# Keys, queries and the product with the convolved rows by high and low parts (three float32r products each) in the third layer of a four-layer kernel

## What is computed

```python
# third layer: B, H, W = 32, 56, 56; C = 96, 6 heads of 16, windows of 7 x 7 (49 tokens), 8 windows in a row
xn = (x - mu) * rsqrt(var + EPS) * norm_gamma + norm_beta
shifted = roll(xn, (-3, -3), (1, 2))
dw = conv_general_dilated(shifted, dw_w, 7x7, feature_group_count=C) + dw_b    # depthwise
qkv = win_partition(shifted) @ qkv_w.T + qkv_b                                 # q, k, v
attn = softmax(q * scale @ k.T + rpb + mask)
out = attn @ v + win_partition(dw)
out = out @ proj_w.T + proj_b
return x + roll(win_reverse(out), (3, 3), (1, 2))
```

## Time and profile before

| | us |
|---|---|
| median of 3 runs (lowest to highest) | 12334.83 (12328.66 to 12345.21) |
| the profiled execution | 12346.31 |
| its span, first to last instruction | 12344.5 |
| PE busy | 11557.4 (94%) |
| PE weight loads busy | 7528.1 (61%) |
| ACT busy | 7537.9 (61%) |
| DVE busy | 7030.2 (57%) |
| POOL busy | 1543.8 (13%) |

### The profile page before, as it was taken

The page is one execution under the profiler, slowest core; times in us unless marked ns, Lnnn a source line. Parts: engine busy times, 40 slices in busy tenths (PEclk is TensorE's granted clock), DMA queues, the critical chain, the costliest instruction groups (busy, mean ns, idle before and its releaser), DMA issues. The chain is left out here.

```text
span 12344.5 us, 381409 instructions
## 1 busy us (share of the span) xinstructions
PE 11557.4 (94%) x153876; PEld 7528.1 (61%) x153876; DVE 7030.2 (57%) x12108; ACT 7537.9 (61%) x12498; POOL 1543.8 (13%) x2308
## 2 busy tenths in 40 slices
PE   6999998899999999999998999998999999999999
PEld 3434443566666666666675667666666666666666
DVE  4444444556556555555446666666555555555555
ACT  4555554566566566566435777776666666666666
POOL 0000000222222222222000000000111111111111
PEclk9999999899999999999999999999999999999999
DMA  1111111122222222222463333333000000000000
GB/s 56 37 36 39 40 39 34 37 46 46 45 45 46 46 44 47 44 47 45 153 216 69 76 75 76 75 75 66 21 21 21 21 21 21 22 21 21 22 21 20
DMA packets 1104420, 602.40 MB, mean 49 GB/s; under 512 B 864651, under 2 KB 1076566, under 8 KB 1099704
## 3 DMA queue, kind: packets, MB, share of 16 engines
q1 hardware_dynamic: 1091496, 553.66, 19.0%
q10 hardware_dynamic: 12288, 38.54, 0.9%
HBM read 308.38 MB, written 282.75 MB: 48 GB/s over the span
## 5 line engine op out<-in xcount | busy, mean ns | idle before, releaser
L950 PEld LDWEIGHTS banks<-L_ident,L_PR 113*113 113x113 f32 x9216 | 1104.5, 180 | 415.6 <-issue 290.1
L1264 DVE COPY L_VB<-banks 49x384 f32<-49x384 f32 x512 | 287.3, 561 | 1859.4 <-PE banks L966 1859.4
L1026 PE MATMUL banks<-L_XN,L_W 97*128 97x392 f32 x3072 | 1249.0, 516 | 13.2 <-DVE L_XN L1339 0.7
L1185 ACT ACTIVATE L_PR<-L_SX 113x588 f32<-113x588 f32 x1536 | 1084.3, 706 | 277.0 <-DVE L_SX L1301 270.5
L950 PE MATMUL banks<-L_ident,L_PR 113*113 113x113 f32 x9216 | 1249.1, 272 | 2.5 <-ACT L_PR L1185 1.8
L1295 DVE TENSOR_REDUCE L_MX<-banks 113x12 f32<-113x588 f32 x1024 | 783.4, 765 | 605.3 <-PE banks L988 605.3
L1169 ACT COPY L_PT<-banks 113x452 f32<-113x452 f32 x1792 | 871.1, 528 | 395.3 <-PE banks L950 395.2
L378 PE MATMUL banks<-scan_XS,scan_W1T 97*96 (+1 forms) x2688 | 1110.2, 551 | 0.0
L1103 PE MATMUL banks<-L_Hd,L_W 128*97 128x392 f32 x3072 | 1097.2, 493 | 0.0
L1005 PE MATMUL banks<-L_VB,L_PT 113*49 113x34 f32 x36864 | 1074.0, 214 | 2.5 <-ACT L_PT L1169 1.0
L1005 PEld LDWEIGHTS banks<-L_VB,L_PT 113*49 113x49 f32 x36864 | 1026.1, 127 | 26.9 <-issue 1.3
(11 more groups left out here) (199 smaller groups left out, 20433.5 us busy)
## 6 DMA issues: line engine op xcount, KB each, us to landing
L_X<-after_L SPq DMA_DIRECT2D x768, 147.0 KB
after_L<-L_X SPq DMA_DIRECT2D x512, 147.0 KB
conv_T<-L_norm_by_phase SPq DMA_DIRECT2D x96, 512.0 KB, 3.3
L_norm_by_phase<-L_XP SPq DMA_DIRECT2D x512, 84.0 KB, 2.2
scan_XT<-in_x SPq DMA_DIRECT2D x33, 1176.0 KB, 7.0
L_norm<-L_XA SPq DMA_DIRECT2D x256, 147.0 KB, 2.0
L_conv<-conv_D ACTq DMA_DIRECT2D x96, 392.0 KB, 3.0
L_XR<-L_norm SPq DMA_DIRECT2D x256, 147.0 KB, 2.2
```

The lines of the kernel that those rows point to most:

```text
L950: mm = pe.transpose(bank(TURN[a])[0:SPAN, (k % 4) * SPAN:(k % 4 + 1) * SPAN], PR[:, st.v if lag else st.u, 2 * k:2 * k + 2, :].rearrange(" ...
L1026: pe.matmul(bank((7, 6, 7)[j])[:, 0:CH], W1[0:C + 1, j * 128:(j + 1) * 128], XN2[:, st.u], start=True, stop=True).then_inc(s[f"fc1_{j}"], 1)
L1185: act.activation(PR[:, u, a, 0:TOK], SX[:, u, a], ACT.Exp).then_inc(s[f"probs{half}"], 1)
```

## The change

In the L2 pass keys, queries and the product with the convolved rows are made in the manner of `conv_pass`. The three weight tiles are split once, ahead of the pass, into a high part and the rest by VectorE (`split_weights`, a block of its own). In each step POOL splits XN of the next chunk into XNH and XNL behind its copy (`to_windows`), and DW of the same chunk into DWH and DWL (`split_convolution`). `by_parts` on PE adds the three products. Values, scores, transposes, heads and `project` stay as they were, and values still read XN. `front` waits for `xn_parts` where it waited for `xn`, `project_convolution` for `dw_parts` where it waited for the load, and the load of DW for `dw_parts` where it waited for `proj`. DWH and DWL have the layout of DW and are read in the same order as DW was.

```diff
+def split_weights(nc, name, parts):
+    with semaphores(nc, name) as sem:
+        rounded = sem("rounded")
+        with nc.Block() as block:
+            @block.vector
+            def _(dve):
+                for whole, high, low in parts:
+                    dve.tensor_copy(high.bitcast(F32R), whole).then_inc(rounded, 1)
+                dve.wait_ge(rounded, len(parts))
+                for whole, high, low in parts:
+                    dve.tensor_tensor(low.bitcast(F32R), whole, high, ALU.subtract)
...
+        if kind == "L2":
+            split_weights(nc, "L2_parts", [(t[0:C + 1], h[0:C + 1], l[0:C + 1]) for t, h, l in ((Wq, WqH, WqL), (Wk, WkH, WkL), (Wp, WpH, WpL))])
...
                     if kind == "L2":
-                        st.wait("proj", lag + 4)
+                        st.wait("dw_parts", lag + 4)
...
+                def by_parts(out, wh, wl, xh, xl, stop=True):
+                    for n, (wt, xt) in enumerate(((wh, xh), (wh, xl), (wl, xh))):
+                        mm = pe.matmul(out, wt.bitcast(F32R), xt.bitcast(F32R), start=(n == 0), stop=(n == 2) and stop)
+                    return mm
...
-                    pe.matmul(bank(K_BANK)[0:C, 0:CH], Wk[0:C + 1, :], XN[:, st.u], start=True, stop=True).then_inc(s["k"], 1)
+                    out = bank(K_BANK)[0:C, 0:CH]
+                    if not mlp:
+                        by_parts(out, WkH[0:C + 1, :], WkL[0:C + 1, :], XNH[:, st.u], XNL[:, st.u]).then_inc(s["k"], 1)
...
                 def project_convolution(st):
-                    st.wait_turn(loaded[st.of4(1)], 1, N_LOADS, 4)
-                    pe.matmul(bank(PROJ_BANK)[0:C + 1, 0:CH], Wp[0:C, :], DW[:, st.of4(1)].rearrange("c p i j -> c i j p"), start=True, stop=False)
+                    st.wait("dw_parts", 1)
+                    raster = lambda t: t[:, st.v].rearrange("c p i j -> c p (i j)").rearrange("c p n -> c n p")
+                    by_parts(bank(PROJ_BANK)[0:C + 1, 0:CH], WpH[0:C, :], WpL[0:C, :], raster(DWH), raster(DWL), False)
...
                 def front(st):
-                    st.wait("xn", 0)
+                    st.wait("xn_parts", 0)
...
                         pool.tensor_copy(seen(XN[0:C, u]), win(XR[:, u])).then_inc(s["xn"], 1)
+                        st.wait("q", lag + 2)
+                        hold(pool, s["xn"], st.value(lag), passed)
+                        pool.tensor_copy(XNH[:, u].bitcast(F32R), XN[:, u]).then_inc(s["xn_high"], 1)
+                        hold(pool, s["xn_high"], st.value(lag), passed)
+                        pool.tensor_tensor(XNL[:, u].bitcast(F32R), XN[:, u], XNH[:, u], ALU.subtract).then_inc(s["xn_parts"], 1)
+                    def split_convolution(st):
+                        st.wait("proj", 2)
+                        hold(pool, loaded[st.of4(0)], (st.t // 4 + 1) * (16 * N_LOADS), passed)
+                        pool.tensor_copy(DWH[:, st.u].bitcast(F32R), DW[:, st.of4(0)]).then_inc(s["dw_high"], 1)
+                        hold(pool, s["dw_high"], st.value(0), passed)
+                        pool.tensor_tensor(DWL[:, st.u].bitcast(F32R), DW[:, st.of4(0)], DWH[:, st.u], ALU.subtract).then_inc(s["dw_parts"], 1)
                     def step(st):
                         if not st.static or st.t + 1 < NCH:
                             to_windows(st, -1, st.v)
+                        if st.f:
+                            split_convolution(st)
```

More of the change, by code:

```diff
@@ L724, in window_pass @@
         if kind == "L2":
+            XNH = sb("XNH", [C + 1, 2, CH]); XNL = sb("XNL", [C + 1, 2, CH])
+            WqH = sb("WqH", [128, C]); WqL = sb("WqL", [128, C]); WkH = sb("WkH", [128, C]); WkL = sb("WkL", [128, C])
+            WpH = sb("WpH", [128, C + 1]); WpL = sb("WpL", [128, C + 1])
+            DWH = sb("DWH", [C, 2, PHASES, WS, JW]); DWL = sb("DWL", [C, 2, PHASES, WS, JW])
             XR = sb("XR", [C, 2, CH]); DW = sb("DW", [C, 4, PHASES, WS, JW])
@@ L799, in window_pass @@
         if kind == "L2":
-            names += ["biased0", "biased1"]
+            names += ["biased0", "biased1", "xn_high", "xn_parts", "dw_high", "dw_parts"]
         if kind == "L3":
@@ L952, in turn @@
                     mm.then_inc(s[f"turned{a}"], 1)
+                def by_parts(out, wh, wl, xh, xl, stop=True):
+                    for n, (wt, xt) in enumerate(((wh, xh), (wh, xl), (wl, xh))):
+                        mm = pe.matmul(out, wt.bitcast(F32R), xt.bitcast(F32R), start=(n == 0), stop=(n == 2) and stop)
+                    return mm
                 def keys(st):
-                    pe.matmul(bank(K_BANK)[0:C, 0:CH], Wk[0:C + 1, :], XN[:, st.u], start=True, stop=True).then_inc(s["k"], 1)
-                def queries(st):
-                    pe.matmul(bank(Q_BANK)[0:C, 0:CH], Wq[0:C + 1, :], XN[:, st.u], start=True, stop=True).then_inc(s["q"], 1)
+                    out = bank(K_BANK)[0:C, 0:CH]
+                    if not mlp:
+                        by_parts(out, WkH[0:C + 1, :], WkL[0:C + 1, :], XNH[:, st.u], XNL[:, st.u]).then_inc(s["k"], 1)
+                    else:
+                        pe.matmul(out, Wk[0:C + 1, :], XN[:, st.u], start=True, stop=True).then_inc(s["k"], 1)
+                def queries(st):
+                    out = bank(Q_BANK)[0:C, 0:CH]
+                    if not mlp:
+                        by_parts(out, WqH[0:C + 1, :], WqL[0:C + 1, :], XNH[:, st.u], XNL[:, st.u]).then_inc(s["q"], 1)
+                    else:
+                        pe.matmul(out, Wq[0:C + 1, :], XN[:, st.u], start=True, stop=True).then_inc(s["q"], 1)
                 def values(st):
```

## The result

| | before | after |
|---|---|---|
| median, five runs each (lowest to highest), us | 12334.83 (12328.2 to 12361.26) | 12438.91 (12414.34 to 12463.53) |
| ratio, 95% interval | | 1.008 (1.0059 to 1.0102) |
| the profiled execution, us | 12346.31 | 12420.84 |
| its span, us | 12344.5 | 12419.1 |

The kernel is 104 us slower; the forecast was 110. **The number of the forecast is right by luck, its mechanism is wrong.** The pass that was changed became faster, and a pass that no line of the change speaks of became slower. Ratios in this document leave out one execution of the kernel before that took 28146.14 us at a mean granted clock of 0.392.

The account below looks back on a forecast made before the run. It took L2 to be bound by a ring through PE and VectorE, 8.03 us a step. 255 x 0.415 = 105.8 us plus 4 gave +110, so 12445 us; range 12395 to 12556.

Parts of the forecast that it names:

- The ring: L2 step's critical cycle: scores to bias, VectorE's run to O, heads_turned, convolved-rows product, turn, project; sum 8.03 us.
- keys and queries at 0: In L2, their single passes save PE 0.2 to 0.3 us, but PE then waits for O; taken as 0.
- heads_turned: PE's turning of the heads after O in each L2 step (L1012), counted as 0.43 us of 8.03.
- The product with the convolved rows, +0.415 us a step: L1018 in L2: three strided single passes at 0.415 us each, 1.245 us in place of 0.83.
- Rival (a): Stride costs L2's single passes nothing new: 0.21 us each, -0.21 a step, 12286 us, faster; chance 0.14.
- The copy of O as a cap: ScalarE's copy before L1022 would cap the gain at about 0.3 us a step if L1018 shrank.
- POOL's splits at 0: POOL's added casts and subtractions in L2: busy 3.3 us a step, at most 3.9, PE never waiting; cost 0.
- Rival (c): POOL's split of DW slows VectorE's X1 and bias in L2: 0.6 us a step more, 12598 us; chance 0.04.
- Once only, +4 us: Ahead of the L2 loop: weight splitting, later first keys and more semaphores to clear, together +4 us.

## Why the prediction was right and wrong

- **The ring, and keys and queries at 0**: right. VectorE's run stayed at 4.41 us, PE's idle time before heads_turned appeared (0.20 to 0.23 us, forecast 0.1 to 0.3), and keys and queries alone moved the step by less than 0.01 us. Not foreseen: together with the other part they are worth 0.12 us a step by way of ScalarE.
- **The product with the convolved rows, +0.415 us a step**: wrong, and this is the step that failed: "I take 0.415 us for each of the three". The reasoning before it was that the stride "limits how fast numbers arrive". Three passes take 0.57 us in place of 0.83. Rival (a) had the part that matters, that the pattern costs a single pass nothing. Its figure was off: it halved the strided record to 0.21 us, and the pass takes 0.165, which is half of the contiguous record (0.33). That a float32 record is two sweeps was not tested. A limit of 1.06 ns on a number cannot hold when the same pattern delivers 392 of them in 0.165 us, 0.42 ns each. The stride's price belongs to float32, whose strided record takes 0.415 and contiguous one 0.33. At the half clock the two were alike; from that I concluded a limit on supply. The runs show a price of the stride for float32 products only, and not what causes it. The run with storage order in the changed kernel excludes a stride price for single passes. Nor was the convolution's 0.205 us a sign of short supply: for 448 columns it is the pace of the contiguous passes here (an estimate, 0.18 x 448 / 392 = 0.206). Why its other passes are 0.23 apart no run here looked for.
- **heads_turned** took 0.43 us in the sum as a fixed term; with a single pass behind it the distance is 0.36, and 0.43 wherever a float32 product follows. With -0.26 for the product this makes -0.33 a step, measured -0.32.
- **The copy of O as a cap "at about 0.3 us a step"**: the mechanism is right. It took hold in the run with the product alone, at 0.21.
- **POOL's splits at 0**: right for the end, wrong in size. POOL was to be busy 3.3 us a step, 3.9 at most. The windows view of the changed kernel has 992.64 us in 1900, 246 steps, 4.0 us, and nobody waits for it in the loop: the view of L980 has PE idle for POOL twice in the whole pass, 19.4 us, which includes the first keys of the pass.
- **Rival (c), POOL against VectorE**: the contention exists and misses the ring. It falls on the subtraction behind O. VectorE and POOL on one timeline:

```profile
7511.99 1.03 DVE L1339 TENSOR_TENSOR L_SX<-L_SR,L_MX 113x588 f32<-113x588 f32 x1
...
7519.69 0.76 DVE L1339 TENSOR_TENSOR L_SX<-L_SR,L_MX 113x588 f32<-113x588 f32 x1
...
7511.88 0.51 POOL L1489 CAST L_XNH<-L_XN 97x392 fp32r<-97x392 f32 x1 [0.17 <-POOL L_XN L1486]
7512.57 1.32 POOL L1491 TENSOR_TENSOR L_XNL<-L_XN,L_XNH 97x392 fp32r<-97x392 f32 x1 [0.18 <-POOL L_XNH L1489]
...
7519.75 1.08 POOL L1489 CAST L_XNH<-L_XN 97x392 fp32r<-97x392 f32 x1 [0.17 <-PE banks L980]
```

  In the first step POOL's cast started 0.11 us before VectorE's subtraction, which took 1.03 us instead of 0.76; in the next VectorE was first, and the cast took 1.08 instead of 0.51. In the run with the product alone, where POOL does not split XN, this subtraction took 0.76 us in every step between 7000 and 8000 us. The operations of the ring before it (bias, maximum, O) kept their durations. The Trainium skill (GPSIMD Engine Reference, "Specifications") says that GpSimd shares its SBUF interfaces with VectorE and contends with its instructions that have two SBUF inputs. The trace agrees: L1339 reads L_SR and L_MX, both in SBUF, and the bias (one input in PSUM) was not lengthened.
- **Once only, +4 us**: about right. From the convolution's last turn to the first keys of the L2 pass it is 2.4 us longer (53.0 to 55.4), and the stretch behind the L2 loop 1.0. The other part of the 7 in the account lies in stretches that the change does not touch, or is balanced by shorter written-out steps.
- **The term that was missing**: +167 us in L3. No step of the prediction priced PE instructions as places in memory; "nothing changes its place; three matmuls of the program have become nine" was true of the order, and not of the addresses. By luck it made up for the wrong sign of the other term: -79 in L2 and +167 in L3. The profiled executions are 75 us apart and the medians 104, since the one lies 11.5 us above its median and the other 18.1 below. The changed kernel's runs spread over 49 us and go with the mean granted clock, from 12414.34 us at 0.976 to 12463.53 at 0.971; with nothing loaded in the loops the spread is 5 to 11 us. The prediction named its own test, "if the strided passes are 0.21 apart (then a)". By that test it fell (they are 0.165 apart), though the total stands inside the range.

The rows before could have shown the danger. The queue "instruction" had 609 packets, all but 61 of them in L1, and keys there stood 307.9 us idle for "issue" against 84.4 in L3, a loop of almost the same length (1714 against 1721) that had no loading at all. Two loops so alike with such different behaviour are a hint that the place matters and that one of them may be near an edge.

## What to carry to other kernels

If a change adds instructions to an engine whose loops are long, look at the engine's instruction queue and at idle time put down to "issue" before explaining the result, and compare the two kernels with their loops equally well placed: here a shift of 67 idle instructions alone was worth +1.5%, and the right ones in the untouched kernel -1.7%, each more than the arithmetic of the change (0.7%). Price a matmul in a new format from a matmul in that format only: what a stride costs in float32 said nothing of a single pass here. And a part that is worth nothing alone can be worth something beside another, when it moves a queue that the other then waits for.

## What the runs showed of the hardware that was not expected

- A PE loop of 1714 or 1721 instructions is fetched anew in each turn or stays in place depending on where it begins: 9 packets of 16.4 KB a turn, and on average 2.5 to 2.9 us (L3) or 3.6 to 4.1 us (L1). For L3 it is none at shifts of 0, 24 and 243 to 256, about half at 52, all at 67 and 72.
- Behind such a load, with PE idle for 1.74 to 1.99 us, the granted clock fell from 1.00 to 0.50 for 3.4 or 10.2 us in 16 of the 61 turns of the changed L3. They lasted 62.34 us in place of 58.89; other turns idled up to 1.95 us and kept their clock.
- Distances of matmuls with 392 columns at a granted clock of 1.00: float32 records 0.33 us contiguous and 0.415 with neighbours 196 numbers apart; single float32r passes 0.18 contiguous and 0.165 so strided, with 0.24 to 0.26 for the first after another kind.
- A `sem_inc` of its own on PE takes 0.15 us.
- VectorE's two-input subtraction and POOL's cast delay each other, whichever comes second: 0.76 to 1.03 us, 0.51 to 1.08 us.
